# Three turn banks in layer 0, another tail order, and the second batch's selection split in two parts

## The reference

```python
x = x + tanh(g_xattn[0]) * attention0(layernorm(x), ctx)   # 16 heads of 8, mask0
x = x + tanh(g_ffn[0]) * ffn0(layernorm(x))     # Hadamard, 4-bit rows, ternary weight
x = x + tanh(g_xattn[1]) * attention1(layernorm(x), ctx)   # 16 heads of 64, mask1
x = x + tanh(g_ffn[1]) * moe(layernorm(x))      # 32 experts of width 64, top 4, shared expert
```

## Time and profile before

| What | Value |
| --- | --- |
| Median of 3 runs | 278.34 us (277.91 to 278.48) |
| The profiled execution, its own time | 278.08 us |
| Its span, first to last instruction | 276.3 us |
| Mean granted clock of TensorE | 0.994 |
| Busy: PE / PEld / DVE / ACT / POOL | 254.2 / 201.0 / 211.6 / 190.9 / 181.0 us |
| Waits of PE between 226 and 240 us | 0.93, 0.41, 1.09 and 0.60 us |
| First gated product of batch 1 | 257.12 us, waited 0.90 us for a DMA |
| Last instruction starts | 273.57 us |

### The profile page before, as it was taken

How to read it: one execution, slowest core, us unless ns; L and a number is a source line. 1 busy time by engine, 2 the same in 40 slices (tenths; PEclk the granted TensorE clock), 3 DMA queues, 4 the chain that set the end, 5 groups by cost and what they waited for, 6 DMA issues and landing times. The chain is left out here.

```text
span 276.3 us, 6695 instructions
## 1 busy us (share of the span) xinstructions
PE 254.2 (92%) x1903; PEld 201.0 (73%) x1903; DVE 211.6 (77%) x654; ACT 190.9 (69%) x454; POOL 181.0 (65%) x271
## 2 busy tenths in 40 slices
PE   7897999999778998989999999999979989799994
PEld 5565766676547786778777788877757767799993
DVE  3999889889959795889677877787797524685683
ACT  3488779888769785857776776776866563656462
POOL 7367999675888675745743685348757794916380
PEclk9999999999999999999999999999999999889999
DMA  6558375100023675635484767676441131301540
GB/s 197 213 165 283 130 266 140 54 2 4 1 66 71 133 153 117 135 88 121 118 217 114 185 165 180 175 180 174 120 97 34 51 108 38 105 13 36 181 115 19
DMA packets 25987, 32.91 MB, mean 119 GB/s; under 512 B 4000, under 2 KB 18144, under 8 KB 25824
## 3 DMA queue, kind: packets, MB, share of 16 engines
q1 hardware_dynamic: 25520, 32.27, 43.5%
q10 hardware_dynamic: 432, 0.22, 0.3%
HBM read 14.32 MB, written 3.47 MB: 64 GB/s over the span
## 5 line engine op out<-in xcount | busy, mean ns | idle before, releaser
L586 POOL TENSOR_SCALAR probs<-probs,rsum 128x512 f32<-128x512 f32 x128 | 87.9, 693 | 59.0 <-DVE rsum L922 58.3
L729 ACT ACTIVATE probs<-masked,neg_max 128x512 f32<-128x512 f32 x128 | 91.8, 718 | 12.7 <-DVE neg_max L913 9.1
L1196 PE MATMUL bank<-ident,probs 128*128 128x128 f32 x512 | 78.5, 276 | 4.0 <-DVE probsT L929 2.5
L1196 PEld LDWEIGHTS bank<-ident,probs 128*128 128x128 f32 x512 | 58.5, 141 | 21.2 <-issue 11.2
L913 DVE CUSTOM_DVE_ANT_0 masked<-bank,mask 128x512 f32<-128x512 f32 x64 | 43.8, 684 | 16.4 <-PE bank L1321 16.0
L737 ACT ACTIVATE probsT<-bank 128x512 f32<-128x512 f32 x74 | 43.4, 587 | 16.5 <-PE bank L1196 16.5
L1348 PE MATMUL bank<-probsT,val 128*32 128x256 f32 (+1 forms) x512 | 46.6, 384 | 0.9 <-ACT mixT L747 0.9
L929 DVE COPY probsT<-bank 128x512 f32<-128x512 f32 x54 | 36.7, 680 | 12.5 <-PE bank L1196 12.3
L913 DVE CUSTOM_DVE_ANT_0 masked<-bank,shared 128x512 f32<-128x512 f32 x64 | 43.3, 676 | 0.4 <-PE bank L1314 0.3
L1348 PEld LDWEIGHTS bank<-probsT,val 128*32 128x32 f32 (+1 forms) x512 | 24.7, 123 | 19.0 <-issue 5.9
L1314 PE MATMUL bank<-parts 128*128 128x512 f32 x64 | 31.3, 489 | 4.4 <-DVE neg_max L913 4.4
(11 more groups left out here) (238 smaller groups left out, 526.9 us busy)
## 6 DMA issues: line engine op xcount, KB each, us to landing
k_both<-k_low SPq DMA_DIRECT2D x32, 128.0 KB, 2.9
k_both<-k_high SPq DMA_DIRECT2D x32, 128.0 KB, 2.8
q<-q_split SPq DMA_DIRECT2D x32, 128.0 KB, 2.4
probsT<-staged_gate SPq DMA_DIRECT2D x32, 128.0 KB, 2.9
q<-q_split SPq DMA_DIRECT2D x32, 64.0 KB, 2.0
parts<-staged_k SPq DMA_DIRECT2D x7, 256.0 KB, 2.7
w_flat<-in_w SPq DMA_DIRECT2D x1, 1536.0 KB, 7.8
staged_k<-k_high SPq DMA_DIRECT2D x2, 512.0 KB, 3.1
```

The lines of the kernel that those rows point to most:

```text
L586: pool.tensor_scalar(p, p, rsum[:, u % NCOL:u % NCOL + 1], 1.0, ALU.mult, ALU.mult).then_inc(normed, 1)
L729: act.activation(probs[:, u % NP, :], masked[:, u % NS, :], ACT.Exp, scale=-1.0, bias=neg_max[:, c:c + 1], accum_out=sums[:, c:c + 1]).the ...
L1196: ins = pe.transpose(dst[0:rows, t * P:t * P + P], src, ident[:, :])
```

## The change

- Layer 0 turns go through three banks (2, 3 and 7) in place of two; layer 1 keeps two. Its copies are counted by three semaphores of their own.
- The output projection of layer 0 becomes a job `("out", b)` in a job bank.
- The last block but one is copied and projected one step earlier, the last projected in the step of its copy; ScalarE takes two attention steps ahead of each even half step.
- The logits of batch 1 get bank 7 to themselves and wait only for the first of the three copies of `ln`.
- The parts of the selection of batch 1 go to other half steps; part 10 is cut off from 8 and 9; ranks move from half step 13 to 15, the gate transposes from 15 to 17. GpSimd takes the power of the variance ahead of two weight splits. ScalarE and VectorE read the `ln` job in its own half step.

```diff
-        self.copy_at = self.mix_at + (2 if layer == 1 and not last else 1)
-        self.out_at = self.copy_at + 1
+        late = layer == 1 and b == B - 1 and g >= self.groups - 2
+        self.copy_at = self.mix_at + (2 if layer == 1 and not late else 1)
+        self.out_at = self.copy_at + (0 if last else 1)
...
-LATE_JOBS = {"ln": 7, "logits": 8, "rank": 13, "turn_gate": 15}
-LATE_ROUTER = {4: (0, 1), 6: (3,), 9: (6,), 10: (8, 9, 10), 13: (12,)}
+LATE_JOBS = {"ln": 7, "logits": 8, "rank": 15, "turn_gate": 17}
+LATE_ROUTER = {3: (0, 1), 5: (3,), 9: (6,), 10: (8, 9), 12: (10,), 15: (12,)}
...
+    for k in (BLOCKS[3], BLOCKS[7]):
+        plan.setdefault(k.out_at, []).append(("out", k.b))
...
-        i = 1 if j in last else number[j] % 2
+        i = 2 if j == ("logits", 1) else 1 if j in last else number[j] % 2
...
+def turn_home(u):
+    return u % 3 if u < L1_AT else u % 2
+def copies_before(i, u):
+    return (u - i + 2) // 3
...
-        job_banks = bank[5:7]
+        turn_bank0 = [bank[2], bank[3], bank[7]]
+        job_banks = bank[5:8]
...
             for e in range(2 * STEPS):
+                if e == 1:
+                    rstd_of(3, 1)
                 for n in WEIGHTS_LATER.get(e, ()):
                     split_weights(n)
-                if e == 1:
-                    rstd_of(3, 1)
                 low_hid(e)
...
-                    if b == 0:
+                    if b == 0 and p % 2 == 0:
                         attend(EXPERTS_AT + p)
+                        attend(EXPERTS_AT + p + 1)
                     for j in AFTER.get(n - 1, ()):
-                        job(j)
+                        if j != ("ln", 3, 1):
+                            job(j)
...
                         act.activation(silu[:, e % 2, 0:wide], u_bank[e % 2][:, 0:wide], ACT.Silu).then_inc(silu_ready, 1)
+                        if n + 1 == LATE_JOBS["ln"]:
+                            job(("ln", 3, 1))
                         for done in HIDDEN_AT.get(e - 1, ()):
                             high_hid(done)
...
-                    for j in AFTER.get(n - 1, ()):
-                        job(j)
+                    for j in AFTER.get(n, ()) + AFTER.get(n - 1, ()):
+                        if (j in AFTER.get(n, ())) == (j == ("ln", 3, 1)):
+                            job(j)
...
+                elif name == "out":
+                    pe.wait_ge(mix_copied, j[1] + 1)
+                    for t in range(NQ):
+                        ins = pe.matmul(job_bank[:, t * P:t * P + P], mixT[:, (j[1] + 1) % 2, t * P:t * P + P], w0T[:, 3, :],
+                                        start=True, stop=True)
...
-                    pe.wait_ge(*freed(("ln", 3, j[1])))
+                    pe.wait_ge(half_done, 2 * j[1] + 1)
+                    if j[1]:
+                        pe.wait_ge(y_used, 2)
...
             def turn(u):
                 pe.wait_ge(normed, u + 1)
-                if u >= 2:
-                    pe.wait_ge(copied[u % 2], u // 2)
+                i = turn_home(u)
+                if u < L1_AT:
+                    if u >= 3:
+                        pe.wait_ge(copied0[i], u // 3)
+                elif u < L1_AT + 2:
+                    pe.wait_ge(copied0[i], copies_before(i, L1_AT))
+                else:
+                    pe.wait_ge(copied[i], (u - L1_AT) // 2)
...
             def down(e):
...
                 if d == 0 and b:
-                    pe.wait_ge(y_used, 4)
+                    pe.wait_ge(*freed(("logits", 1)))
```

More of the change, by code:

```diff
@@ L154, in make_plan @@
             highs[j] = count
+    after = {o: tuple(js) for o, js in after.items()}
     return before, plan, after, number, place, highs
@@ L370, in build @@
         copied = [sem("copied0"), sem("copied1")]
+        copied0 = [sem(f"copied0_{i}") for i in range(3)]
         mixed = sem("mixed")
@@ L898, in add_y @@
                 x = x_sb[:, NQ * b:NQ * b + NQ, :]
-                y = (moe_bank[0][:, 0:SQ] if layer == 2 else y_bank[:, b * SQ:b * SQ + SQ]).rearrange("p (t c) -> p t c", c=P)
+                y = (job_banks[PLACE["out", b][0]][:, 0:SQ] if layer == 0 else moe_bank[0][:, 0:SQ] if layer == 2
+                     else y_bank[:, b * SQ:b * SQ + SQ]).rearrange("p (t c) -> p t c", c=P)
+                used, n = freed(("out", b)) if layer == 0 else (y_used, 2 * layer + b - 1)
                 if layer < 2:
@@ L902, in add_y @@
                 dve.scalar_tensor_tensor(out=x, in0=y, scalar=tanh_g[:, gate:gate + 1], in1=x,
-                                         op0=ALU.mult, op1=ALU.add).then_inc(y_used, 1)
-                dve.wait_ge(y_used, 2 * layer + b + 1)
+                                         op0=ALU.mult, op1=ALU.add).then_inc(used, 1)
+                dve.wait_ge(used, n)
             def mask_max(u):
@@ L1061, in router @@
                 if o == 0:
-                    dve.wait_ge(projected_out, B + 8 * b + 8)
+                    dve.wait_ge(projected_out, 8 * b + 8)
                     add_y(1, b, 1)
@@ L1324, in turn @@
                 pe.wait_ge(normed, u + 1)
[L1325 to L1332 removed]
+                i = turn_home(u)
+                if u < L1_AT:
[5 more added lines that the diff above has]
+                    pe.wait_ge(copied[i], (u - L1_AT) // 2)
+                turn_tiles((turn_bank0 if u < L1_AT else turn_bank)[i], [probs[:, u % NP, n * P:n * P + P] for n in range(NK)]).then_inc(turned, 1)
+            def mix(k):
+                if k.layer:
+                    for i in range(2):
+                        pe.wait_ge(copied[i], (k.end - L1_AT) // 2)
+                else:
+                    for i in range(3):
+                        pe.wait_ge(copied0[i], copies_before(i, k.end))
                 if k.layer == 0:
@@ L1354, in project_out @@
                 pe.wait_ge(mix_copied, n)
-                if k.layer == 1 and k.g == 0:
+                if k.g == 0:
                     pe.wait_ge(ld["bo1"], 32)
-                if (k.layer == 0 or k.g == 0) and (k.layer or k.b):
-                    pe.wait_ge(y_used, 2 * k.layer + k.b)
+                    if k.b:
+                        pe.wait_ge(y_used, 1)
+                    else:
+                        pe.wait_ge(copied0[2], copies_before(2, L1_AT))
                 for t in range(NQ):
@@ L1361, in project_out @@
                     ins = pe.matmul(y_bank[:, c:c + P], mixT[:, n % 2, t * P:t * P + P],
-                                    w1_out[:, k.g, :] if k.layer else w0T[:, 3, :],
-                                    start=((k.layer == 0 or k.g == 0) and t == 0),
+                                    w1_out[:, k.g, :], start=(k.g == 0 and t == 0),
                                     stop=(k.g == k.groups - 1), skip_group_check=True)
@@ L1387, in attend @@
                         mix(k)
-                    if t == k.out_at and (k.layer or k.g == 3):
+                    if t == k.out_at and k.layer:
                         project_out(k)
```

35 lines of the change are left out of this document (20 added, 15 removed).

## The result

The changed kernel took 280.68 us (median of 5 runs, 279.68 to 280.98), the kernel before 278.34 beside it (277.81 to 278.48): a ratio of 1.0077, 95% interval 1.0057 to 1.0097. The profiled execution is the median one, 280.68, span 278.8, against 278.08 and 276.3 before.

A forecast was written before the change was run, and what follows sets the result against it. Two paths, PE's own work and the gates, were taken to set the end. Layer 0: 0, tail +0.7, clock +0.3 on 278.08 gave 279.1, or 279.3 with the median's 0.26; range 276.8 to 280.6 us.

The forecast's parts named there:

- rival D: In the tail, the low clock costs in full: +0.7 and +1.7, time 280.7 us; chance 0.06.
- Layer 0, 0: Layer 0's three turn banks and output job gain nothing, since the next score matmul still waits for VectorE's maximum: 0.
- Rival C: In layer 0, the third bank pays: all 2.5 us of waits gained, time 276.8 us; chance 0.14.
- Tail order, faster on PE but not at the end: End of attention: earlier mix copy and last projection shorten PE's waits (0.93, 0.41), but the end follows the gates.
- Logits bank: End of attention: logits' own bank shrinks PE's waits of 1.09 and 0.60 to at most 0.3.
- Gate path, steps 1 to 6: Tail, from residual add to gate copy: summed in the new order, gate copy at 251.8 instead of 251.11, 0.7 later.
- Step 4, the block: Selection's second part, behind step 5's pair: blocked by GpSimd's subtraction, takes 2.7 us (bounds 1.25 and 2.9).
- Step 6, the move of the gate copy: Gate copy on ScalarE moves behind silu 9 and step 8's high part: at 251.8 instead of 251.11.
- Clock, +0.3: Tail, PE idle some 3 us before step 12's second product: clock falls again, costing 0.3 (bounds 0 to 1.7).
- three signs that I had named: Tail: gate copy between 251.4 and 252.4; PE idle 2 us or more before step 12's second product; PEclk under 1 behind.
- the end follows the gates, +0.7: Tail sum: gates come 0.7 us later, and the kernel's end moves later with them by +0.7.

The follow-up runs named there:

- the fastest: Changed kernel with selection, ranks and gates in their earlier half steps, and step 4's hidden block copied only after silu 6: 275.96 us, ratio 0.9913.
- the old places: Changed kernel with batch 1's part 10 back beside 8 and 9 in half step 10, ranks in 13, gate transposes in 15: 276.68 us, ratio 0.9951.
- the filled kernel: Changed kernel with useless PE products, 11 before the ranks and 14 before the second product of step 12: 279.77 us, ratio 1.0055.
- the late copy: ScalarE copies step 4's hidden block only after silu 6: 277.31 us (0.9975) on the kernel before, 275.96 us (0.9913) with the old places.
- the code moved: Changed kernel with 120 added PE waits on a semaphore long reached, moving later code 120 instructions on: 280.90 us, ratio 1.0105.

## Why the prediction was right in direction and 1.4 us short

**How near it was.** The median, 280.68 against the forecast 279.3, lies 0.1 past the end of the range, 280.6; the ratio times 278.34 gives 280.5, just within it. It is also the number of rival D, 280.7, but the profile does not show D's mechanism: the clock did not fall behind the last wait. So that the range reached this far is in part luck: it was drawn for D's sake.

**Layer 0, 0:** right. Alone it gave 1.0003, and two banks in place of three changed neither the changed kernel nor the fastest. Rival C is out: its 2.5 us went to waits on the maximum.

**Tail order, faster on PE but not at the end:** right for the changed kernel; with the old places it is worth 0.5%, which I did not list as what the part could bring by itself. **Logits bank:** no effect of its own.

**Gate path, steps 1 to 6.** Forecast and trace: residual add 231.0 and 231.72; end of step 3's pair 238.3 and 239.23; table load 238.9 and 239.92; end of step 5's pair 244.2 and 245.35; selection 246.9 and 247.94; gated product of step 7 249.5 and 250.41; gate copy 251.8 and 252.80. The length of the path from the add on was 20.8 forecast and 21.1 measured. 0.74 of the constant 1.0 is layer 1 running later, which stood at the first k copy of ScalarE already (7.07 us against 5.94) and is no doing of the schedule: in the kernels with the same layer 0 the reference mix lay anywhere from 222.76 to 224.53. From the mix the gates came 0.95 later, where I had 0.7.

**Step 4, the block:** right in place, cause and size. Part 10 took 2.68 us from 245.26 to 247.94 where I took 2.7, and the path to the selection became 1.0 shorter with GpSimd's work moved (old places) and 1.3 with it cut (changed kernel). VectorE's operations there read and write SBUF alone; its products, which read a PSUM bank, kept 0.69 beside a subtraction (244.66). By the rule of the Trainium skill that the prediction named ("SBUF — State Buffer", "SBUF: two separate sides"), the traces agree.

**Step 6, the move of the gate copy:** right. The half step back gave 1.1.

**Clock, +0.3:** right in size as far as the profile tells, wrong in place. I had it behind the wait for the first gated product. It fell behind the 1.33 us wait for the selection, which I had not seen: I let PE reach the ranks with the selection ready, and put all idle time at step 12. PE stood there 1.84, not 3, since it came there at 258.45 and not near 255. From the ranks on, its products took 10.4 us, where I had 7 to 8; with the clock up (the filled kernel) they took 8.9. The rate of 48 in 5 us came from a window in which seven of the 48 were the short matmuls of the ranks. So three signs that I had named did not come: the gate copy was at 252.80, past 252.4; PE was idle for less than 2 us at step 12; and PEclk behind it was 1.00. Rival D's full price does occur: 2.1 in one execution with two banks.

**The step that failed is the tail sum's "the end follows the gates, +0.7"**, in its sizes. That the end follows the gated product holds for these two kernels (19.18 and 19.25 us); with the old places, where PE no longer waits for the gates, the way is 20.09. But I carried the DMA's leg over from one execution as a constant, 6.70 from gate copy to the end of the gated product; it was 7.44 in the profiled run. The 14 profiled kernels show 3.55 to 4.96 us for its part behind the first load (4.14 before, 4.88 after). The time of the reference mix is another 1.8 us wide. So of 2.5 us between the two profiles 1.02 belong to the path (0.95 and 0.07), as forecast (1.0), and twice 0.74 to terms which vary by more than that. The median was also 280.68, so some of this is there in typical executions; which part is lasting, these runs do not settle. A hint: the five profiles of the changed tail with gates at 17 and part 10 late have the leg at 4.83 to 4.96 four times and at 3.88 once, the shortest run of its kernel; the others have 3.55 to 4.14. The slow second load, told above, is how it comes about; what makes it slow is not shown.

**Why the old places are faster** follows from the same legs. The change took PE's early waits away (3.03 us) but VectorE and ScalarE still had the selection to make. Put late, it leaves PE filled now and starved later, at two places (the ranks and step 12), each with a chance of the lower clock; put early, PE waits 2.15 once and never again for the gates, because they come 3.1 us sooner. With the late copy the two paths nearly meet again: the gated product waits 0.53 for its rows and PE waits 1.13 for the ranks.

## What to carry to other kernels

When an engine's waits are removed upstream, spend what is won on the chain that feeds the end, not on filling the engine: the gates were 0.95 us later with PE relieved of 3.03. Look for small VectorE operations that take five times their usual span and for the GpSimd operation that ends just then; moving its producer behind one more ScalarE operation won 0.7 and 1.1 us in two kernels, by the ratios. And give a store and load through DRAM on the critical path a range, not the duration of one trace.

## What the runs showed of the hardware

- The first load of gate rows to the gated product that needs two of them took 3.55 to 4.96 us in 14 profiled kernels, with the queue's issues at the same distance (1.85 to 1.87 us from gate copy to first load).
- The lower clock is not a matter of the length of a wait alone. It followed waits of PE of 1.33 us (0.89 and 0.77 in the next two stretches of 5 us), of 1.32 in the kernels with the gates at 16 (0.88, 0.77) and with the code moved (0.78, 0.88), of 2.8 (0.82, 0.84) and of 2.98 (0.50, 0.85). It did not follow one of 2.15 with the old places (mean 1.000), nor that of 1.32 for the selection with two banks. Four waits alike within 0.01 us (0.93, 0.41, 1.09 and 0.60) were followed by 0.66 in the kernel before and by 1.00 in that kernel with the late copy.
- A VectorE operation over 64 columns, all in SBUF, that was blocked by a subtraction of GpSimd for its full length took 1.22 to 1.31 us in place of 0.22, and ended within 0.1 us of it.
- Of the loads of gate rows, 2.8 to 3.4 us from issue to landing in most cases, single ones took 3.6 to 4.2. In 13 of 14 profiles the first such load was issued close to the start of a code transfer.
